# A split first expert layer for the late tiles of a macaron block on one Trainium2 core

## The reference

```python
x = layer_norm(src + attention(src), ln1_g, ln1_b)      # 16 heads of 8
keys = (x @ router_w + router_b)[..., 0]
expert_idx = remainder(floor(keys), 4)
for e in range(4):
    h = relu(x @ W1[e] + b1[e])                          # 128 -> 512
    y = h @ W2[e] + b2[e]                                # 512 -> 128
    ff_out += where(expert_idx == e, y, 0)
return layer_norm(x + ff_out, ln2_g, ln2_b)
```

## Time and profile before

| | |
|---|---|
| median of 3 runs | 881.33 us (880.96 to 882.14) |
| profiled execution | 881.06 us, span 879.2 us |
| TensorE products | 816.1 us busy, 93% of the span |
| VectorE | 721.4 us, 82% |
| ScalarE | 648.6 us, 74% |
| GpSimd | 539.5 us, 61% |
| mean granted TensorE clock | 0.988 of full speed |
| moved by DMA | 83.53 MB |

### The profile page before, as it was taken

One profiled execution on the slowest core, in us unless ns is written; L12 is line 12 of the kernel. 1 busy time (PEld: TensorE's weight loads), 2 busy tenths in 40 slices (PEclk: granted clock), 3 DMA queues, 4 the chain that ended last, 5 costly groups with the idle time before them and its releaser, 6 DMA issues.

```text
span 879.2 us, 26036 instructions
## 1 busy us (share of the span) xinstructions
PE 816.1 (93%) x8477; PEld 613.6 (70%) x8477; DVE 721.4 (82%) x1819; ACT 648.6 (74%) x1242; POOL 539.5 (61%) x914
## 2 busy tenths in 40 slices
PE   7999999999989889789999989999999999989893
PEld 6666666666657879667787767666666666658793
DVE  4889999989896857489989877898998999967775
ACT  2888888888976668345554656988888888876783
POOL 4235776767738655537777773366776767566755
PEclk9999999999999999899999999999999999999997
DMA  9994599200005565300000000000000000045561
GB/s 278 368 414 95 87 399 412 90 24 12 18 21 160 146 178 164 89 24 1 0 0 0 1 2 1 2 2 25 12 18 18 12 24 12 13 120 162 176 178 40
DMA packets 40724, 83.53 MB, mean 95 GB/s; under 512 B 5160, under 2 KB 25406, under 8 KB 36172
## 3 DMA queue, kind: packets, MB, share of 16 engines
q1 hardware_dynamic: 35148, 70.01, 25.2%
q0 software_dynamic: 5504, 12.63, 3.9%
HBM read 32.63 MB, written 51.04 MB: 95 GB/s over the span
## 4 chain that ended last, share of the span: by engine, by line
PE 64%; DVE 12%; issue 10%; POOL 9%; ACT 2%; DMA 1%; DVEq 0%; POOLq 0%; SPq 0%; ACTq 0%
PE duo L651 10%; PE duo L594 10%; DVE mx L1359 7%; PE duo L739 4%; PE duo L587 4%; POOL out L1938 4%; PE duo L725 3%; PE duo L902 3%; PE duo L632 2%; PE duo L588 2%; PE duo L881 2%; PE duo L570 2%; PE duo L547 2%; PE duo L890 2%; PE duo L634 2%
## 5 line engine op out<-in xcount | busy, mean ns | idle before, releaser
L1359 DVE TENSOR_REDUCE mx<-duo 128x4 fp32r<-128x1024 f32 x256 | 313.6, 1225 | 48.9 <-PE duo L594 41.4
L1072 ACT ACTIVATE probs<-duo 128x1024 f32<-128x1024 f32 x256 | 263.0, 1028 | 33.2 <-PE duo L600 24.7
L594 PE MATMUL duo<-stacks 32*128 32x256 f32 x1024 | 128.1, 327 | 18.2 <-DVE mx L1359 14.2
L651 PE MATMUL duo<-probs,v_st 128*32 128x256 f32 x2048 | 137.3, 385 | 0.5
L600 PE MATMUL duo<-q_st,stacks 32*128 32x256 f32 x1024 | 128.3, 328 | 0.1
L594 PEld LDWEIGHTS duo<-stacks 32*128 32x128 f32 x1024 | 76.6, 183 | 60.1 <-DVE mx L1359 27.6
L1058 ACT ACTIVATE stacks<-duo,small 128x512 fp32r<-128x512 f32 x128 | 88.8, 694 | 7.6 <-PE duo L588 7.0
L651 PEld LDWEIGHTS duo<-probs,v_st 128*32 128x32 f32 x2048 | 53.5, 109 | 40.2 <-ACT probs L1072 1.4
L587 PE MATMUL duo<-qk_hi,sel_r 128*128 128x256 f32 x256 | 78.7, 329 | 2.0 <-DVE qk_lo L1348 1.6
L739 PE MATMUL duo<-w,xs 128*128 x608 | 75.8, 279 | 4.5 <-DVE hidden L1529 2.7
L739 PEld LDWEIGHTS duo<-w,xs 128*128 128x128 f32 x608 | 73.5, 193 | 8.9 <-issue 7.0
(11 more groups left out here) (217 smaller groups left out, 1909.2 us busy)
## 6 DMA issues: line engine op xcount, KB each, us to landing
x_sorted<-ret SPq DMA_DIRECT2D x2, 17476.0 KB, 51.9
wbuf<-in_W SPq DMA_DIRECT2D x38, 256.0 KB
ret<-x_sorted SPq DMA_DIRECT2D x22, 257.0 KB, 3.2
stacks<-x_sorted SPq DMA_DIRECT2D x12, 257.0 KB, 3.0
wside<-w_pack SPq DMA_DIRECT2D x38, 66.0 KB
decay_rows<-prow SPq DMA_DIRECT2D x1, 1536.0 KB
xs<-x_sorted SPq DMA_DIRECT2D x4, 257.0 KB, 2.8
rows<-in_c_sel_ffn SPq DMA_DIRECT2D x1, 1024.0 KB, 7.0
```

The source lines that it names most:

```text
L594: return pe.matmul(score_bank[h % 2][:, t * SEQ:(t + 1) * SEQ], q_st[r:r + 32, g, t * P:(t + 1) * P], k_st[r:r + 32, g, :], start=True, st ...
L651: last = pe.matmul(into[32 * j:32 * j + 32, :], v_st[:, half, t, first:first + VC], probs[:, (g * GH + j) % RING, t, :], start=(t == 0 and ...
L1072: act.activation(probs[:, h % RING:h % RING + 2, :, :], duo_now[:].rearrange("p (n t q) -> p n t q", n=2, t=TT), ACT.Exp, scale=SCALE).the ...
L1359: dve.tensor_reduce(rows, score_duo[:].rearrange("p (n t k) -> p n t k", n=2, t=TT), AX.X, ALU.max, negate=True).then_inc(max_done, 1)
```

## The change

For tiles 6 to 18 of both expert stages the first layer is no longer an fp32 product. x and W1 are each split in a high part, rounded to fp32r, and a remainder, and three fp32r products (low W1 by high x, high W1 by low x, high by high) are summed in the same bank. Tiles 0 to 5 stay as they were, with a buffer of their own, `wplain`. W1 is split once: SP loads it early into the space of the decay masks; GpSimd makes high part and remainder of two experts after batch 1 of the first attention and of the other two after batch 3; SP writes them to `w_pack` in DRAM, from which the late tiles load 512 KB instead of 256. ScalarE's copy of x becomes the high part; VectorE makes the remainder from PSUM (`split_x`), at the head of each pass of its tile loop. TensorE's transposes then wait for the remainder two tiles back (one tile back in tiles before 8) where they waited for the copy. VectorE keeps `late_b2`.

```diff
-PACK = CPE + DM
+PACK = 2 * DFF + CPE + DM
+WHOLE = 6
-        wbuf = sb("wbuf", [P, 3, DFF])
+        wbuf = sb("wbuf", [P, 3, 2 * DFF], FP32R)
+        wplain = sb("wplain", [P, 3, DFF])
+        w1_stage = dm_flat[:, 0:2048]
+        x_hi = sb("x_hi", [P, 2, SEQ], FP32R)
+        x_lo = sb("x_lo", [P, 2, SEQ], FP32R)
...
+        def lo_count(ph, k):
+            return ph * (TILES - WHOLE) + k - WHOLE + 1
...
             sp.dma_start(xs[:, 2:4], xv[:, 2:4]).then_inc(ld_xs, 16)
+            sp.dma_start(w1_stage.rearrange("p (e n) -> p e n", e=NE), A["W1"].rearrange("e d n -> d e n")).then_inc(ld_e, 16)
...
             clear_rows(0)
+            sp.wait_ge(pk_ready, 1)
+            sp.dma_start(w_pack[0:2, :, 0:2 * DFF].rearrange("e p n -> p e n"), wbuf[:, 0:2, :].bitcast(FP32)).then_inc(pk_half, 16)
...
             sp.wait_ge(set_scr, 16)
 
+            sp.wait_ge(pk_ready, 2)
+            sp.dma_start(w_pack[2:4, :, 0:2 * DFF].rearrange("e p n -> p e n"), wbuf[:, 0:2, :].bitcast(FP32)).then_inc(pk_half, 16)
...
-                    sp.dma_start(wbuf[:, n % 3, :], A["W1"][bass.ds(e, 1), :, :].rearrange("e d n -> d (e n)")).then_inc(wt_in[n % 3], 16)
-                    sp.dma_start(wside[:, n % 3, :], w_pack[bass.ds(e, 1), :, :].rearrange("e p n -> p (e n)")).then_inc(wt_in[n % 3], 16)
+                    if k < WHOLE:
+                        sp.dma_start(wplain[:, n % 3, :], A["W1"][bass.ds(e, 1), :, :].rearrange("e d n -> d (e n)")).then_inc(wt_in[n % 3], 16)
+                    else:
+                        sp.dma_start(wbuf[:, n % 3, :].bitcast(FP32), w_pack[bass.ds(e, 1), :, 0:2 * DFF].rearrange("e p n -> p (e n)")).then_inc(wt_in[n % 3], 16)
+                    sp.dma_start(wside[:, n % 3, :], w_pack[bass.ds(e, 1), :, 2 * DFF:PACK].rearrange("e p n -> p (e n)")).then_inc(wt_in[n % 3], 16)
...
-                    wait(pe, xd_ready, n if k < EARLY else n - 1)
+                    held = k - 1 if k < EARLY else k - 2
+                    if held < WHOLE:
+                        wait(pe, xd_ready, first + held + 1)
+                    else:
+                        pe.wait_ge(xlo_ready, lo_count(ph, held))
...
-                    pe.wait_ge(xd_ready, n + 1)
+                    if k < WHOLE:
+                        pe.wait_ge(xd_ready, n + 1)
+                    else:
+                        pe.wait_ge(xlo_ready, lo_count(ph, k))
                     for c in range(CPE):
                         wait(pe, h_ready, 4 * (n - 1) + c + 1)
+                        o = bank[c][:, 0:SEQ]
+                        hi, lo = (wbuf[:, n % 3, m * DFF + c * P:m * DFF + (c + 1) * P] for m in range(2))
...
+                            pe.matmul(o, lo, x_hi[:, n % 2, :], start=True, stop=False)
+                            pe.matmul(o, hi, x_lo[:, n % 2, :], start=False, stop=False)
+                            pe.matmul(o, hi, x_hi[:, n % 2, :], start=False, stop=True).then_inc(up_ps, 1)
...
-                    act.activation(x_dims[:, n % 2, :], rows_bank(k)[:, 0:SEQ], ACT.Copy).then_inc(xd_ready, 1)
+                    act.activation((x_dims if k < WHOLE else x_hi)[:, n % 2, :], rows_bank(k)[:, 0:SEQ], ACT.Copy).then_inc(xd_ready, 1)
...
+                def split_x(k):
+                    n = first + k
+                    dve.wait_ge(xd_ready, n + 1)
+                    dve.wait_ge(up_ps, 4 * (n - 1))
+                    dve.tensor_tensor(x_lo[:, n % 2, :], rows_bank(k)[:, 0:SEQ], x_hi[:, n % 2, :].bitcast(FP32), ALU.subtract).then_inc(xlo_ready, 1)
...
                 for k in range(5, TILES + 2):
+                    if k + 1 < TILES:
+                        split_x(k + 1)
                     moments(k - 2)
...
+            def pack(half):
+                if half == 0:
+                    pool.wait_ge(ld_e, N_LDE)
+                else:
+                    pool.wait_ge(pk_half, 16)
+                for n in range(2):
+                    block = w1_stage[:, (2 * half + n) * DFF:(2 * half + n + 1) * DFF]
+                    pool.tensor_copy(wbuf[:, n, 0:DFF], block).then_inc(pk_hi, 1)
+                for n in range(2):
+                    block = w1_stage[:, (2 * half + n) * DFF:(2 * half + n + 1) * DFF]
+                    pool.wait_ge(pk_hi, 2 * half + n + 1)
+                    last = pool.tensor_tensor(wbuf[:, n, DFF:2 * DFF], block, wbuf[:, n, 0:DFF].bitcast(FP32), ALU.subtract)
+                last.then_inc(pk_ready, 1)
...
                     if live(i, base):
                         place_v(i, 1)
+                    if i == 1:
+                        pack(0)
                     if i == 3:
+                        pack(1)
```

More of the change, by code:

```diff
@@ L461, in _ @@
             for e in range(NE):
-                sp.dma_start(w_pack[e, :, CPE:PACK], A["b2"][e].partition_broadcast(P)).then_inc(pk_out, 16)
+                sp.dma_start(w_pack[e, :, 2 * DFF + CPE:PACK], A["b2"][e].partition_broadcast(P)).then_inc(pk_out, 16)
             sp.wait_ge(set_act, 1)
-            sp.dma_start(w_pack[:, :, 0:CPE].rearrange("e p n -> p e n"),
+            sp.dma_start(w_pack[:, :, 2 * DFF:2 * DFF + CPE].rearrange("e p n -> p e n"),
                          bias_cols[:, 0:CHUNKS].rearrange("p (e n) -> p e n", e=NE)).then_inc(pk_out, 16)
@@ L476, in _ @@
             clear_rows(1)
+            sp.wait_ge(pk_half, 32)
             sp.wait_ge(pk_out, 16 * (NE + 1))
@@ L531, in _ @@
             experts(1)
-        N_LDB, N_LDE = 2 * 16, 16
+        N_LDB, N_LDE = 2 * 16, 2 * 16
         SET_ATT, SET_DVE = 6, 29
@@ L1546, in finish @@
                     dve.tensor_tensor(yo[:, n % 3], zn[:, n % 2], xt[k % XT_RING][:, :, DM:2 * DM], ALU.add).then_inc(yo_ready, 1)
-                return late_b2, add_ffn, moments, finish
+                return split_x, late_b2, add_ffn, moments, finish
             def experts(ph, attend):
                 base = ph * BATCH
-                late_b2, add_ffn, moments, finish = tiles(ph)
+                split_x, late_b2, add_ffn, moments, finish = tiles(ph)
                 attend(base + 16, slots(0, 5))
```

8 lines of the change are left out of this document (5 added, 3 removed).

## The result

| | before | after |
|---|---|---|
| median | 883.02 us (20 runs) | 889.80 us (20 runs) |
| profiled execution | 881.06 us, span 879.2 | 892.69 us, span 890.1 |
| ratio, with its 95% interval | | 1.0062 (1.0038 to 1.0086) |
| VectorE busy | 721.4 us | 733.7 us |
| mean granted TensorE clock | 0.988 | 0.979 |

The change makes the kernel slower by some 6 us (the medians differ by 6.8, the ratio is worth 5.5); 877.1 was forecast. The two profiled executions above lie 10.9 us apart in span, more than the change is worth; a second pair of traces further down has 6.1. Single executions scatter by more than 1%, so this text reads positions in the traces, and compares whole times only between kernels that ran on one chip.

The account below looks back on a forecast made before the run. TensorE was taken to set the pace of tiles 8 to 18 at 3.73 us each. Terms -8.2 + 1.4 + 2.4 + 0.2 = -4.2 us gave 877.1 us against the median, range 873.5 to 881.5.

Parts of the forecast that it names:

- Packing W1: First attention: GpSimd's first half hidden in idle time, second half delays later GpSimd work; +0.2 us, bounds 0 and 1.9.
- The weight loads of the late tiles: Expert stages: 512 KB land 3.5 us behind issue, so late issues show; +1.2 us a stage, bounds 0 and 3.1.
- The first layer: Tiles 6 to 18: twelve fp32r products take 1.36 us instead of 1.73; period 3.36 us, -8.2 us for both stages.
- VectorE's remainder: Tiles from 6 on: one more subtraction per tile makes VectorE's period 3.37 us, hidden with nothing to spare.
- Ahead of tile 9: Expert stages: remainder of tile 6 (0.4 us) and larger weight load (0.3) make tile 9 late; 0.7 us a stage.
- rival 2: Late tiles: slower weight loads bring the period back to 3.73 us and delay tile 9; 885 us, chance 0.08.
- rival 1: Late tiles: weight loads set a period of 3.59 us, so no change overall; 881.4 us, chance 0.14.
- Rival 3: Stage two, tiles 7 and 9: TensorE's clock falls behind the new waits, kernel still faster; chance 0.08.
- Sum: Whole kernel: -8.2 + 1.4 + 2.4 + 0.2 = -4.2 us, giving 877.1 us against the median.
- GpSimd stopped at the second half: First attention: first half's write lands late, so GpSimd waits over 4 us before packing the second half; chance 0.04.
- The chance of slower: Whole kernel: probability 0.12 that the change makes it slower, against faster 0.72 and same 0.16.

Follow-up runs that it names:

- d3_whole_moved: Changed kernel with all W1 packing, in its large 128x512 operations, moved to the head of batch 2 of the first attention: 885.60 us (one run).
- d1_after: The changed kernel run again with nothing altered, for a second trace: 888.21 us.
- b1_before: The kernel before the change run again with nothing altered, for another trace: 882.22 us.
- c4_split_from_8: Changed kernel with tiles 6 and 7 unsplit as well, so the split starts at tile 8, nothing else: 899.90 us (one run).
- b2_half_weights: Changed kernel whose late tiles load only W1's high part (256 KB, not 512) and use it as remainder too: 882.78 us against 884.18 before, ratio 0.9994.
- b4_combo: Changed kernel with 128x128 packing, second half in batch 2, earlier W1 loads, tile 9 ahead of tile 8's weights, split from tile 8: 878.62 us against 884.18 before.
- d4_combo2: Changed kernel with smaller, moved packing, earlier W1, split from tile 8, tile 9 before tile 8's weights, its weights before tile 10's rows: 875.89 us against 883.75 before.

## Why the prediction was wrong, point by point

**The step that failed: "Packing W1", +0.2 us, and beside it the size of "The weight loads of the late tiles".** Against the forecast the first is worth 4.9 us, the second about 4.5. The packing first. The step asked which work of GpSimd the packing delays, found idle time of GpSimd for it, and called the first half hidden (a half took 3.7 us for the 4.1 forecast). That part was right: no late result of GpSimd is what TensorE waits for. What it left out is that GpSimd's work can hold up VectorE without any wait in the program. Batch 1 cost 2.2 us in stall and 0, 1.4 or 2.8 by the clock, batch 3 about 1.2. The Trainium skill, "GPSIMD Engine Reference", section "Specifications", says that GpSimd shares its SBUF interfaces with VectorE, "contention with DVE instructions in a 2-port perf mode or with two SBUF inputs". The traces agree: scalar operations, casts and two-input operations on SBUF are stretched (0.14 to 1.28 us), reductions out of PSUM (1.23) and a one-input reduction out of SBUF (0.41) are not. Which of the two conditions holds for the scalar operations and the casts no trace shows. That the hold lasts until GpSimd's running instruction ends, in d3_whole_moved the next one too, is read from these traces.

**The first layer.** 1.36 was forecast. The twelve products start 0.12 us apart with a longer first gap (860.27 to 861.75), 1.48 us; the period is 3.41, not 3.36. The gain is 0.32 a tile and not 0.37: 11 tiles in each of two stages give 7.0 us, not 8.2.

**VectorE's remainder.** Hidden, as forecast, in the late tiles: 0.42 us long, and behind it VectorE waits for TensorE again (0.38 us at 860.33). The forecast had nothing to spare there.

**Ahead of tile 9.** +0.7 a stage was forecast; +0.8 and +0.9 came in the first trace, +0.7 and +1.0 in d1_after against b1_before. The wait before tile 7 came with 2.5 us for the 2.6 forecast, and the wait for tile 9 swallowed it (c4_split_from_8). That the forecast 0.7 came may be luck: neither taking the remainders away (c4_split_from_8) nor halving the bytes (b2_half_weights) brought tile 9 back, so neither of its two terms is shown, and the place is open.

**The weight loads.** +1.2 us a stage was forecast, out of a landing 3.5 us behind the issue. In the tiles that waited it was 4.1 to 5.5, in d1_after up to 5.8. From tile 9 to 18 nine periods of 3.41 would be 30.7 us; d1_after has 34.7 and 33.6, so late weights take 4.0 and 2.9. That is 6.9 us for the 2.4 forecast, nearly three times what I took; in these nine tiles the split gives only 2.9 a stage. In the first trace it is 3.8 and 3.7, after taking off 1.6 for the lower clock behind tile 9 of stage one. Three of the four lie above the forecast's bound of 3.1, for which it has no row. Without the second 256 KB tile 9 to 18 takes 32.2 and 31.6 us (b2_half_weights), so these bytes are 2.5 and 2.0 us of d1_after's; the rest, 1.5 and 0.9, is late even with 256 KB. The mechanism was right, the size wrong: the landing was an estimate at the rate of the busiest quarter microsecond. The tiles came out nearer to rival 2 (3.6 us slower) than to rival 1 (no change): +2.7, in single late tiles and not in a longer period.

**The clock.** Rival 3 had it right that the clock falls behind the new waits. It named tile 7 and 9 of stage two; there the first trace shows 1.00 and d1_after a fall behind tile 7. In stage one both traces have one there. The wait for tile 9 hides it. The costly one was in attention, behind a stall that was not foreseen. After that stall of 2.15 to 2.44 us the clock fell in six of seven traces.

**Sum.** Against the forecast of -4.2 the second pair of traces has +6.1: attention gives +5.1 for +0.2, the stretches from tile 0 to 18 +2.7 for the tiles' -4.4, and the rest is -1.8. In that rest stand the first layers of tiles 17 and 18 of both stages, worth -1.3 of the -7.0; the remaining -0.5 the change does not touch.

The chance of "GpSimd stopped at the second half", 0.04, was for another mechanism and did not occur: GpSimd never waited for the transfer of the first half. The chance of slower, 0.12, was too small: no rival had GpSimd's work lengthen VectorE's. The forecast also counts from 881.33, the median of three executions; over 20 it is 883.02.

## What to carry to other kernels

Before work is put into an idle time of GpSimd, read what VectorE does in the same microseconds: small operations on SBUF in front of a result that TensorE needs are the bad case, reductions out of PSUM kept their length here. Bytes that are loaded per tile have a landing time that must be measured from issue to use, not taken from the peak rate. A split that doubles a load gave its gain here only when the load was also issued earlier and in another order (b4_combo, d4_combo2).

## What the runs showed that was not expected

- An operation of VectorE on one number a partition takes 1.28 us beside a 128x512 subtraction of GpSimd and 0.14 without it; one took 2.03 us beside two in a row.
- Pieces of 128x128 shorten the hold-up but make GpSimd's work longer: 5.3 us for 3.7.
- The same stall of TensorE (2.15 to 2.44 us) is followed by a granted clock of 1.00, 0.86 or 0.72 over the next 12 us, from one execution to another; a good part of the scatter of this kernel is of that kind.
- Two of the four chips of the groups have the kernel before at 893 to 896 us instead of 884, and the traces from them show waits in the expert stages, of up to 4.3 us ahead of tile 9, that those of the other two don't have at this size. Their cause is open and wasn't tried.
